# Near keys of a strided attention in 64x64 tiles, with the near unit ahead of the near scores

## The reference

```python
STRIDE = 4
LOCAL = 8
def _strided_allowed(S):
    i = jnp.arange(S)[:, None]
    j = jnp.arange(S)[None, :]
    return (j % STRIDE == 0) | (jnp.abs(i - j) <= LOCAL)
...
scores = jnp.einsum('bhqd,bhkd->bhqk', q, k) / jnp.sqrt(jnp.asarray(D, x.dtype))
allowed = _strided_allowed(S)
scores = jnp.where(allowed, scores, -jnp.inf)
attn = jax.nn.softmax(scores, axis=-1)
out = jnp.einsum('bhqk,bhkd->bhqd', attn, v)
out = out.transpose(0, 2, 1, 3).reshape(B, S, H)
return out @ o_w + o_b
```

## Time and profile before

| what | us |
|---|---|
| median of 3 runs (1086.38 to 1088.70) | 1087.83 |
| the profiled execution | 1086.01 |
| its span in the profile | 1084.2 |
| attention's 64 steps within it, about | 206 to 1025 |

### The profile page before, as it was taken

The page is one execution under the profiler, slowest core; times in us unless marked ns, Lnnn a source line. Parts: engine busy times, 40 slices in busy tenths (PEclk is TensorE's granted clock), DMA queues, the critical chain, the costliest instruction groups (busy, mean ns, idle before and its releaser), DMA issues.

```text
span 1084.2 us, 27687 instructions
## 1 busy us (share of the span) xinstructions
PE 1028.3 (95%) x10694; PEld 462.7 (43%) x10695; DVE 933.8 (86%) x1162; ACT 839.8 (77%) x1590; POOL 251.2 (23%) x387
## 2 busy tenths in 40 slices
PE   4999999699999999999999999999999999999898
PEld 2666666233333333333333333333333333333487
DVE  6989897889999999999999999999999999999133
ACT  4667674288888888888888888888888888888600
POOL 2444453012212121221212122212121222212100
PEclk9999999599999999999999999999999999999999
DMA  6787878213223333333333333323343332231166
GB/s 197 227 254 252 262 250 274 54 46 88 85 83 90 98 85 93 102 91 99 97 96 109 98 99 95 104 84 108 91 113 88 105 91 82 86 85 58 48 236 239
DMA packets 166777, 134.07 MB, mean 124 GB/s; under 512 B 70492, under 2 KB 145884, under 8 KB 166636
## 3 DMA queue, kind: packets, MB, share of 16 engines
q1 hardware_dynamic: 163912, 128.06, 39.3%
q10 hardware_dynamic: 2736, 4.26, 1.2%
HBM read 71.13 MB, written 59.84 MB: 121 GB/s over the span
## 4 chain that ended last, share of the span: by engine, by line
PE 76%; DVE 12%; issue 7%; DMA 2%; ACT 2%; DVEq 0%; ACTq 0%
PE ps_attend L1228 17%; PE ps_attend L1145 12%; DVE peak_far L1087 10%; PE ps_attend L1186 10%; PE ps_project L621 7%; PE ps_attend L1235 6%; PE ps_attend L1308 5%; PE ps_attend L1156 4%; PE ps_project L679 4%; PE ps_attend L1197 3%; PE ps_project L594 3%; PE ps_attend L1163 3%; PE ps_attend L1204 2%; DMA sums<-out_rows 2%; PE ps_project L656 1%
## 5 line engine op out<-in xcount | busy, mean ns | idle before, releaser
L1087 DVE TENSOR_REDUCE peak_far<-ps_attend 128x2 f32<-128x1024 f32 x512 | 608.5, 1220 | 41.0 <-PE ps_attend L1186 30.8
L1028 ACT ACTIVATE probs<-ps_attend 128x512 f32<-128x512 f32 x1024 | 541.1, 597 | 49.5 <-PE ps_attend L1145 46.3
L1228 PE MATMUL ps_attend<-probs,v_op 128*17 128x512 f32 x2048 | 270.1, 600 | 0.5 <-issue 0.5
L1145 PE MATMUL ps_attend<-q_op,k_op 51*128 51x512 f16 x1024 | 252.1, 387 | 4.9 <-ACT probs L1028 3.3
L1186 PE MATMUL ps_attend<-k_op,q_op 48*128 48x512 f16 x1024 | 189.6, 388 | 26.1 <-DVE peak_far L1087 15.5
L1033 ACT ACTIVATE probs<-ps_attend 108x512 f32<-108x512 f32 x256 | 138.7, 594 | 34.6 <-PE ps_attend L1163 34.6
L1145 PEld LDWEIGHTS ps_attend<-q_op,k_op 51*128 51x128 f16 x1024 | 76.8, 93 | 193.9 <-ACT probs L1028 137.4
L894 POOL CAST negmax<-peak 128x16 bf16<-128x16 f32 x64 | 12.6, 196 | 609.6 <-DVE peak L1070 609.6
L1090 DVE TENSOR_REDUCE peak_near<-ps_attend 128x8 f32<-128x864 f32 x128 | 131.0, 1023 | 10.5 <-PE ps_attend L1204 10.4
L885 POOL TENSOR_TENSOR out_rows<-out_rows,share_rows 128x512 f32<-128x512 f32 x64 | 81.4, 1272 | 66.1 <-DMA share_rows<-shares_dram 64.0
L621 PE MATMUL ps_project<-xT_parts,w_parts 128*128 128x512 f16 x384 | 90.6, 387 | 2.1 <-DVE xT_parts L465 2.1
(11 more groups left out here) (91 smaller groups left out, 937.4 us busy)
## 6 DMA issues: line engine op xcount, KB each, us to landing
share_rows<-shares_dram SPq DMA_DIRECT2D x64, 256.0 KB
attn_dram<-out_rows SPq DMA_DIRECT2D x64, 256.0 KB, 5.5
q_dram<-qk_parts SPq DMA_DIRECT2D x48, 256.0 KB, 4.7
k_dram<-qk_parts SPq DMA_DIRECT2D x48, 256.0 KB, 2.7
q_op<-q_dram SPq DMA_DIRECT2D x128, 96.0 KB, 2.4
k_op<-k_dram SPq DMA_DIRECT2D x64, 144.0 KB, 3.1
v_dram<-v_sb SPq DMA_DIRECT2D x16, 544.0 KB, 3.0
base<-in_x SPq DMA_DIRECT2D x16, 512.0 KB, 4.7
```

What stands on the lines that cost most here:

```text
L1028: ins = nc.scalar.activation(probs[:, r, h], ps_s[st.bank(kind)], ACT.Exp, scale=undo)
L1087: ins = nc.vector.tensor_reduce(peak_far[:, :, p, tile], banks, AX_X, ALU.max)
L1145: nc.tensor.matmul(bank, k[half(f, KM), keys], q[half(f, KM), p], start=True, stop=True).then_inc(s_ready, 1)
L1228: ins = nc.tensor.matmul(ps_o[h * VW:h * VW + VR], v[:, r, h * VR:(h + 1) * VR], probs[:, r, h], start=(r == 0), stop=False)
```

## The change

The near keys of both passes go into 64x64 tiles of the array. A tile of 128 queries is cut into two halves of 64 (`SUB`), and each half has its own window of 60 near keys (`NEAR`). The two halves go to two column halves of the array, the two heads stay in the two row halves, so that four tiles stand side by side. One near unit a step takes the place of two, and one near score pair (two banks) the place of two (four banks); ScalarE's near exponentials go from four of 108 partitions to two of 128. The mask is the same for every window, so `mask_q` and `mask_k` shrink to three arrays of one tile's pattern (`near_q`, `near_k`, `near_one`). Round 4 weighs 8 blocks of 64 queries in place of 4 of 128. V for near keys is laid out by halves of 64 partitions with zeros between (`v_zeroed`: two memsets on GpSimd), and comes by six small DMAs and one large an iteration in place of three and one. The keys of the two pairs are laid out with their far keys inward; the pads at the outer ends are copies of far keys, made on GpSimd by four small copies an iteration (`set_edges`), for which TensorE waits before a near unit of a new iteration (`edges_ready`). `AHEAD` is 4, `TURN` stays 8.

The core of the diff:

```diff
-BANDS = ((1, 18), (6, 6), (21, 5))
+SUB = HALF
+NEAR = (SUB + 2 * LOCAL) // STRIDE * (STRIDE - 1)
+SUB_STEP = SUB // STRIDE * (STRIDE - 1)
+NEAR_BANDS = ((1, 16), (4, 6), (12, 5))
...
+def strided(u):
+    return WPAD + (S if u else S - NS)
+def places(u):
+    return WPAD + u * (S + NS)
...
-UNITS = TT * PAIRS + TT // 2
+UNITS = TT * PAIRS + 1
-AHEAD = 5
+AHEAD = 4
 SCORE_PAIRS = (
     ("far", 0, 0), ("far", 0, 1), ("far", 2, 1), ("far", 1, 0), ("far", 1, 1),
     ("near", 0), ("far", 2, 0), ("negmax",), ("far", 3, 1), ("far", 3, 0),
-    ("near", 1),
 )
 MAXIMA = (
-    ("far", 2, 1), ("far", 1, 0), ("far", 0, 0), ("near", 0), ("far", 2, 0),
-    ("far", 3, 1), ("far", 1, 1), ("far", 3, 0), ("near", 1), ("far", 0, 1),
+    ("far", 2, 1), ("far", 1, 0), ("far", 0, 0), ("far", 2, 0),
+    ("far", 3, 1), ("near",), ("far", 1, 1), ("far", 3, 0), ("far", 0, 1),
 )
...
+        def set_edges(st):
+            k, it = k_op[st.parity(2)], st.iteration(2)
+            pool.wait_ge(k_loaded[st.parity(2)], 16 * 2 * 2 * PAIRS * (st.half_iteration(2) + 1))
+            edges = ((0, strided(0)), (SK - WPAD, strided(1)))
+            for i, (f, (to, of)) in enumerate(itertools.product(range(2), edges)):
+                nc.gpsimd.tensor_copy(k[half(f), to:to + WPAD], k[half(f), of:of + WPAD]).then_inc(edges_ready, 1)
+                pool.wait_ge(edges_ready, 4 * it + i + 1)
+        pool.wait_ge(done["y8_ready"], B * CPB)
+        set_edges(Step(0, FIRST))
...
+        nc.gpsimd.memset(v_op[1][:, NS // P:, :], 0.0).then_inc(v_zeroed, 1)
...
-                r = 2 * (place - 2) + piece - 1
-                load_v(it, par, range(r, r + 1))
+                r = 2 * (2 * (place - 2) + piece) - 1
+                load_v(it, par, range(max(r - 1, -1), r + 1))
...
-                    ins = nc.scalar.activation(probs[0:WIN, ROUNDS - 1, h], ps_s[st.bank(kind)][0:WIN], ACT.Exp,
-                                               scale=undo)
+                    ins = nc.scalar.activation(probs[:, ROUNDS - 1, h], ps_s[st.bank(kind)], ACT.Exp, scale=undo)
...
-        def score_near(st, i):
+        def score_near(st):
+            banks = [free_score(st, ("near", f)) for f in range(2)]
+            for sub, f in itertools.product(range(2), range(2)):
+                nc.tensor.matmul(banks[f][half(sub, SUB)], near_one[half(f)], near_q[half(f)], start=True, stop=False)
+            for p, t in itertools.product(range(PAIRS), range(TT)):
+                for sub, f in itertools.product(range(2), range(2)):
+                    at = window(p, st.queries() * TT + t) + sub * SUB_STEP
+                    to = (p * TT + t) * SUB
+                    ins = nc.tensor.matmul(banks[f][half(sub, NEAR), to:to + SUB], k[half(f, KM), at:at + NEAR],
+                                           q[half(f, KM), p, t * P + sub * SUB:t * P + (sub + 1) * SUB], start=False,
+                                           stop=(p == PAIRS - 1 and t == TT - 1))
...
+            if st.queries(2) == 0:
+                pe.wait_ge(edges_ready, 4 * (st.iteration(2) + 1))
...
-                for t in tiles:
-                    tile = NS // P + st.queries(d) * TT + t
+                for t, sub in itertools.product(tiles, range(2)):
+                    block = NS // P + 2 * (st.queries(d) * TT + t) + sub
                     for h in range(HG):
-                        ins = nc.tensor.matmul(ps_o[h * VW:h * VW + VR, t * P:(t + 1) * P],
-                                               v[0:WIN, tile, h * VR:(h + 1) * VR],
-                                               near_probs(h, t),
-                                               start=False, stop=(t == TT - 1))
+                        at, to = (h // 2 * TT + t) * SUB, t * P + sub * SUB
+                        ins = nc.tensor.matmul(ps_o[h * VW:h * VW + VR, to:to + SUB], v[:, block, h * VR:(h + 1) * VR],
+                                               probs[:, r, h % 2, at:at + SUB], start=False,
+                                               stop=(t == TT - 1 and sub == 1))
```

More of the change, by code:

```diff
@@ L885, in body @@
                 nc.gpsimd.tensor_tensor(rows, rows, share_rows[:], ALU.mult).then_inc(attn_ready, 1)
+            if st.n >= 0 and st.exists(2) and st.queries(2) == 0:
+                if st.exists(-3):
+                    pool.wait_ge(attn_ready, st.at(-2))
+                set_edges(st)
             if st.exists(1):
@@ L907, in sync_attend, with load_v @@
     def sync_attend(sp):
-        def load_v(it, par, windows=range(-1, STRIDE - 1)):
+        def load_v(it, par, windows=range(-1, 2 * (STRIDE - 1))):
             v = dram["v"][it // G, :, it % G * HG * VR:(it % G + 1) * HG * VR]
+            sp.wait_ge(v_zeroed, par + 1)
             for r in windows:
@@ L1210, in near_probs @@
-        def near_probs(h, t):
-            at = (t % 2 * PAIRS + h // 2) * P
-            return probs[0:WIN, ROUNDS - 1, t // 2 * 2 + h % 2, at:at + P]
+            for sub, f in itertools.product(range(2), range(2)):
+                nc.tensor.matmul(banks[f][half(sub, SUB), 0:PAIRS * TT * NEAR], near_q[half(f), 0:SUB],
+                                 near_k[half(f)],
+                                 start=True, stop=False)
+            for p, t in itertools.product(range(PAIRS), range(TT)):
+                for sub, f in itertools.product(range(2), range(2)):
+                    at = window(p, st.queries(2) * TT + t) + sub * SUB_STEP
+                    to = (p * TT + t) * NEAR
+                    ins = nc.tensor.matmul(banks[f][half(sub, SUB), to:to + NEAR],
+                                           q[half(f), p, t * P + sub * SUB:t * P + (sub + 1) * SUB],
+                                           k[half(f), at:at + NEAR], start=False,
+                                           stop=(p == PAIRS - 1 and t == TT - 1))
+                    if p == PAIRS - 1 and t == TT - 1 and sub == 1:
+                        ins.then_inc(u_ready, 1)
@@ L1223, in weigh @@
                 else:
-                    nc.tensor.matmul(ps_o, keep["ident_bf"][:], mask_k[:, 0:CH], start=True, stop=True)
+                    nc.tensor.matmul(ps_o, keep["ident_bf"][:], near_q[:], start=True, stop=True)
             if r < ROUNDS - 1:
@@ L1244, in far_unit, with near_unit @@
                 unit(st, ("far", tile, p))
-            def near_unit(tiles):
-                unit(st, ("near", tiles))
+            def near_unit():
+                unit(st, ("near",))
             def far(r, p):
@@ L1251, in far, with near @@
                     score_far(st, r, p)
[L1253 removed]
+            def near():
                 if st.exists():
[L1255 removed]
+                    score_near(st)
             def maxima():
```

145 lines of the change are left out of this document (52 added, 93 removed).

## The result

The kernel after the change takes **1104.16 us** in the median of five runs (1097.58 to 1106.88), the kernel before 1087.37 beside it: a ratio, estimated from all runs, of 1.0148, with a 95% interval of 1.0121 to 1.0176. The forecast was 1090, slower, with a range of 1066 to 1116.

What follows compares the result with a forecast made beforehand. TensorE's chain and the DMA round trip of the maxima bound the step; +5.7 for the steps, -2 for waits and -1 ahead made +2.7 on the profiled 1086.0, or 1090 from the median 1087.83, range 1066 to 1116.

Steps and rivals of the forecast that it cites:

- The chain: TensorE's order behind round 4: near unit puts 0.49 us ahead of near scores, near exponentials, last weighting round and maxima.
- Stretch A: TensorE from the matmul of the maxima to the next step's first far scores: 3.58 us falls to 3.44, giving 0.14.
- The step: One steady step, from one maxima matmul to the next: 12.68 us for 12.59, 0.09 more on 63 steps, +5.7 us.
- the trip: Maxima through ScalarE and two DMAs issued by SyncE, which the first far scores await: a floor of 3.44 us.
- stretch B: TensorE from the first far scores to the next maxima, 9.01 us before: takes 0.23 more.
- a group: Four small 64x64 matmuls side by side in a near block: 0.035 us taken; 0.027 to 0.045 gives 1082 to 1100.
- 1111: Rival, 20%: weight loads of the small tiles don't hide, 0.055 us a group, 0.32 a step on top of the layout.
- 1146: Rival, 5%: the four tiles run one behind the other, 0.09 us a group, 0.88 on top of the layout.
- 1179: Rival, 3%: a floor of 0.0225 us for each matmul, round 4 at 1.54, 1.41 on top of the layout.
- the waits for sums: VectorE's 11 waits for the sums, 32.0 us before, now stand where it has some 0.6 us to spare: -2 us.
- ahead of and behind these steps: Ahead of the first maxima, one near reduction less: -1 us.
- Round 4: Weighting of near blocks on TensorE, same columns in twice the instructions: 1.01 us, at least 1.00, at most 1.54.

Runs made afterwards that it cites:

- e10_before_pool_queue: Kernel before the change, with the second of the two DMAs of the maxima issued by GpSimd instead of SyncE: 1084.17 us, ratio to before 0.9977.
- e9_pool_queue: Kernel after the change, with the second of the two DMAs of the maxima issued by GpSimd instead of SyncE: 1079.36 us, ratio to before 0.9925.
- e1_swap: Kernel after the change, with near scores put in front of the near unit behind round 4: 1077.22 us, ratio to before 0.9923.
- e6_even: Kernel after the change, plus 40 tiny matmul instructions and one already met wait in each step, and 22 instructions once in the first: 1097.48 us.
- e8_odd: Same as e6_even but without the 22 instructions in the first step: 1123.33 us, ratio to before 1.0329.

## Why the prediction was right, and what it lacked

**The chain, as drawn.** Stretch A: 3.44 forecast, 3.36 measured, ended by the DMA 61 times, 56.8 us of waiting. The step: 12.68 forecast, 12.67 measured; e10_before_pool_queue and e9_pool_queue show that the trip binds only after, e1_swap that the near unit ahead of the near scores is what stretch B pays. VectorE 10.95 and ScalarE 10.39 a step stand at the forecast 11 and 10.2.

**The tiles.** Eight groups of four take 512.42 - 512.12 = 0.30 behind the masks, 0.0375 a group, for 0.035 forecast; near unit 0.53 for 0.49, near scores 0.58 for 0.51. So at this price the weight loads hide and the four tiles run side by side; the rivals at 1111, 1146 and 1179 didn't happen, though 1111 lies nearer to the time. The 25 ns of the Trainium skill ("TensorE: Matmul & The Clock Gate", Part 1) don't hold across four tiles: 32 matmuls in 0.30 us are 9 ns each.

**The term that was mis-sized.** The sum on the profiled execution was +2.7 and came out as +11.6. By parts: the quiet step +0.08 on the 60 steps between the 3rd and the 63rd maxima, +4.8 (5.4 forecast for these); other irregular steps about 0 (-2 forecast, for the waits for sums); ahead of and behind these steps -3.0 (-1 forecast); and **+9.8 of long stops, for which the sum had nothing.** That is what the trace holds; e6_even, where the stops are gone and other steps grew, shows that taking them away does not give all of it back. Round 4 was priced as "the same columns in twice the instructions" and the near blocks by columns and loads; that instructions must be brought in as well was not asked. The page of the profile of before had the row that raises the question (q8, 85 packets in a span of 1084 us), and the instructions of a step could be counted from the trace.

**What was luck.** Without the stops the parts add up to +1.8 us on the profiled execution, which is hardly a slower kernel. That the measured time lies clearly on the side that was forecast, and well within the range, is owed in the main to a cost that the sum did not have; the range was made for another uncertainty, the price of a group.

**What stays open.** The median of after is 6.6 us above its profiled execution, whose time is the lowest of the five. Stops of one place vary from none to 1.45 us between steps, so runs may differ by them. The granted clock points the same way: 0.986 in the profiled execution, 0.978 to 0.980 in the other four, and in the traces it falls behind stops. But no trace of a slower run shows it. e10_before_pool_queue's 0.23% less than before, at the same quiet step, lies at the edge of what can be told.

## What to carry to other kernels

When a change takes work off the stretch that covers a transfer's round trip, look for the next thing to put there first: here the near unit in the idle 0.85 us turned a loss of 1.5% into a gain of 2.15%, with the same instructions. What produces a value for the next engine goes ahead of what doesn't, and 0.53 us of misplaced work cost about that much in each step. Count instructions as well as columns: some 270 within 2 us ran TensorE out of instructions at one place of a block of 256, 209 did not, and a stop that no semaphore ends, at a fixed number modulo 256, is how it shows. Look at the granted clock behind each stop, since it can add to the price.

## What the runs showed of the hardware

- TensorE's instructions come in packets of 16 KB, 256 at a time. In the 24 stops of after and e8_odd it was 2.2 to 3.1 us from a packet's start until TensorE went on, and 1.2 to 1.5 from its end; TensorE stood until then.
- Where a burst lies in its block decides: with the first load of round 4 at 185 to 221 of 256 TensorE stopped 10 times of 11 in after and 14 of 15 in e8_odd, at 39, 103, 167 and 231 never; the same program shifted by 22 instructions took 26 us less.
- TensorE's granted clock can fall behind such a stop: to 0.66 over the stretch A behind a stop of 1.84 us, which took 4.51 us for 3.40 at full clock.
- A DMA issue holds ScalarE 0.87 us from its copy to the next exponential; on SyncE a pair of issues lasts 1.54 in a quiet step, on GpSimd one took 0.61.
- Four 64x64 matmuls of 60 or 64 columns side by side took 0.0375 us, eight groups in 0.30, weight loads included.
